# Sixteen rows of the first input pair are loaded ahead of the weights

## The chip, the cores and the metric

The kernel runs on one core of one Trainium2 chip. The metric is the device time of one execution in microseconds; the median of 3 runs of the kernel before is 133.78 us (133.74 to 133.89). The core has TensorE (PE), VectorE (DVE), ScalarE (ACT), GpSimd (POOL) and SyncE (SP), and 16 DMA engines that carry the transfers which SP issues.

## The reference, cut to what matters

The reference is a factorisation machine with a small network on its embedding, for 1024 samples of 12500 features:

```python
x_reg = input_data @ W_lin.T + b_lin                     # (1024, 1)
emb = input_data @ factors                               # (1024, 16)
sum_squared = jnp.square(emb.sum(axis=1))
squared_sum = (jnp.square(input_data) @ jnp.square(factors)).sum(axis=1)
h = jax.nn.relu(emb @ W1.T + b1)                         # 128
h = jax.nn.relu(h @ W2.T + b2)                           # 64
dnn_out = h @ W3.T + b3
x = x_reg + 0.5 * (sum_squared - squared_sum)[:, None] + dnn_out
return (0.5 + jax.nn.sigmoid(x) * 5.0).squeeze()
```

All is float32. The input alone has 1024 x 12500 x 4 = 51.2 MB, and each of its elements is used once as it is and once squared.

## The kernel before, in words

The input is transposed on the host, so that features lie on partitions. 97 chunks of 128 features and a rest of 84 features make up the 12500. The first chunk (`xf`) and the rest (`xl`) are loaded on their own; the other 96 chunks are taken in groups of 8 chunks by 512 samples: first all 12 groups of samples 0 to 511, then 8 groups of samples 512 to 1023, and the last 32 chunks of samples 512 to 1023 in 9 smaller pieces (`x_end`). A group is 128 partitions by 4096 numbers, that is 16 KB to a partition.

For every group ACT and DVE square the 8 chunks (3 by DVE, 5 by ACT; lines 327 and 427) into `sq`, POOL places the weights of the group (lines 307 and 308), and PE multiplies: eight matmuls of the input with `wr` and eight of the squares with `wz`, all adding into one PSUM bank (`add_mm`, line 506). After samples 0 to 511 the small network is run for them while the second half is loaded.

All loads are issued by SP, in the order of the code (lines 265 to 285): the head `hd` (all weights and parameters, 128 rows of 7616 bytes), `xf` (128 rows of 4096 bytes), `xl` (128 rows of 3072 bytes), then eight transfers of two groups each, here called pairs (128 rows of 32 KB, 4 MB), then four single groups and nine end pieces. `xr` has six slots of one group. The first three pairs are issued at once; each later one waits (line 272) until PE has used the squares of the groups whose slots it takes (`sq_used`). In `x_pairs`, row p of a pair holds what goes to partition p.

A transfer adds 16 to its semaphore when it has landed. The three pairs of slots have one semaphore each (`x_landed`), and `landed` (line 231) waits for 16 for each round of the six slots. Before pair 0, PE does 4 matmuls on `xf` and 24 on `xl`, then as many on their squares; they need `hd`, `xf`, `xl` and the sums over squared weights that DVE makes from `hd` (lines 410 to 417).

Of the kernel before, what the change touches and what calls it, by code (L numbers as in the profile page):

```python
# [14 lines left out]
P = 128  # L15
# [9 lines left out]
HALF = B // 2  # L25
CHUNKS = 8
TWO = 2
# [7 lines left out]
PAIRED = 16  # L35
# [10 lines left out]


BY_DVE = 3

# [34 lines left out]
def fm_kernel(nc, head, x_first, x_rest, x_pairs, x_groups, x_end, out):  # L86
    with ExitStack() as ctx:
        def sb(name, shape, dt=F32):
            return ctx.enter_context(nc.sbuf_tensor(name, shape, dt))
# [4 lines left out]
        def sem(name):  # L94
            return ctx.enter_context(nc.semaphore(name))
# [4 lines left out]
        xr = sb("xr", [P, SLOTS, CHUNKS, HALF])  # L100
# [35 lines left out]
        x_landed = [sem(f"x_landed{t}") for t in range(SLOTS // TWO)]  # L136
# [40 lines left out]
        def cols(k):  # L177

            c, n = BLOCKS[k]
            return slice(c, c + n)  # L180
# [16 lines left out]
        def line(k):  # L197

            c, n = BLOCKS[k]
            return slice(c // 4, (c + n) // 4)  # L200
# [8 lines left out]
        def width(i):  # L209
            return BLOCKS[PIECES[i][0]][1]  # L210
# [4 lines left out]
        def piece(i, c, n):  # L215

            at = ENDS * (BLOCKS[PIECES[i][0]][0] - HALF)
            return xe[:, at + c * width(i):at + (c + n) * width(i)]
# [8 lines left out]
        def ring(s):  # L227

            return (s + RING - TOTAL) % RING

        def landed(engine, r, s):

            engine.wait_ge(x_landed[s // TWO], 16 * (r + 1))

        def single(engine, g):
            engine.wait_ge(single_landed[g - PAIRED], 16)
# [1 line left out]
        def chunks(i):  # L238
            return sum(PIECES[i][2]) + sum(PIECES[i][3])

        def last_slot(i):
            k, c = PIECES[i][:2]
            return (ENDS * (BLOCKS[k][0] - HALF) + (c + chunks(i)) * BLOCKS[k][1] - 1) // (CHUNKS * HALF)
# [18 lines left out]

        @block.sync
        def _(sp):
            sp.dma_start(hd[:, :], head).then_inc(hd_landed, 16)  # L265
            sp.dma_start(xf[:, :], x_first).then_inc(first_landed, 16)  # L266
            sp.dma_start(xl[:, :, :].rearrange("p c b -> p (c b)"), x_rest).then_inc(rest_landed, 16)  # L267
            for p in range(PAIRED // TWO):
                at = TWO * p % SLOTS
                if TWO * p >= SLOTS:  # L270

                    sp.wait_ge(sq_used, RING + TWO * p + TWO - SLOTS)
                sp.dma_start(xr[:, at:at + TWO].rearrange("p s c b -> p (s c b)"),  # L273
                             x_pairs[p, :, 0:TWO * CHUNKS * HALF]).then_inc(x_landed[at // TWO], 16)
            for g in range(PAIRED, TOTAL):
                sp.wait_ge(sq_used, RING + g + 1 - SLOTS)
                sp.dma_start(xr[:, g % SLOTS].rearrange("p c b -> p (c b)"),
                             x_groups[g - PAIRED, :, 0:CHUNKS * HALF]).then_inc(single_landed[g - PAIRED], 16)
            at = 0
            for i in range(len(PIECES)):  # L280
                c, n = PIECES[i][1], chunks(i)
                rows = x_end[at:at + P * n * width(i)].rearrange("(p m) -> p m", p=P)
                sp.wait_ge(sq_used, RING + TOTAL - SLOTS + END_SLOT + last_slot(i) + 1)
                sp.dma_start(piece(i, c, n), rows).then_inc(end_landed[i], 16)
                at += P * n * width(i)

            for k in range(len(BLOCKS)):
                sp.wait_ge(y_ready[k], 1)
                sp.dma_start(out[cols(k)].rearrange("(q b) -> q b", q=4), y[0:P:32, line(k)]).then_inc(y_stored, 16)
            sp.wait_ge(y_stored, 16 * len(BLOCKS))  # L290
# [27 lines left out]
        def _(act):  # L318
# [5 lines left out]
            def squares(r, s):  # L324

                act.wait_ge(sq_used, SLOTS * r + s + 1)
                nc.scalar.activation(sq[:, ring(s), BY_DVE:CHUNKS, :], xr[:, s, BY_DVE:CHUNKS, :],  # L327
                                     ACT.Square).then_inc(act_squared, 1)
# [30 lines left out]
            with act.Fori(0, GROUPS // SLOTS) as r:  # L359
                for s in range(SLOTS):  # L360
                    landed(act, r, s)
                    squares(r, s)
# [9 lines left out]
            for g in range(GROUPS, PAIRED):  # L372
                landed(act, g // SLOTS, g % SLOTS)
                squares(g // SLOTS, g % SLOTS)
# [32 lines left out]
        def _(dve):  # L407
# [16 lines left out]
            def squares(r, s):  # L424

                dve.wait_ge(sq_used, SLOTS * r + s + 1)
                nc.vector.tensor_tensor(sq[:, ring(s), 0:BY_DVE, :], xr[:, s, 0:BY_DVE, :], xr[:, s, 0:BY_DVE, :],  # L427
                                        ALU.mult).then_inc(dve_squared, 1)
# [33 lines left out]
            with dve.Fori(0, GROUPS // SLOTS) as r:  # L462
                for s in range(SLOTS):
                    landed(dve, r, s)
                    squares(r, s)
# [38 lines left out]
        def _(pe):  # L504
            def add_mm(out, lhsT, rhs):
                return nc.tensor.matmul(out, lhsT, rhs, start=False, stop=False, skip_group_check=True)  # L506
# [12 lines left out]
            def quad(ps, t, m, c, n):  # L519
                return ps[32 * (t % 4):32 * (t % 4) + m, c:c + n]  # L520
# [29 lines left out]
            def add_squares(r, s, h):  # L550
                g = SLOTS * r + s
                pe.wait_ge(wz_ready, g + 1)
                pe.wait_ge(dve_squared, g + 1)
                for c in range(BY_DVE):
                    add_mm(quad(p_lin[h], c, WZ, 0, HALF), wz[:, ring(s), c, :], sq[:, ring(s), c, :])
                pe.wait_ge(act_squared, g + 1)
                for c in range(BY_DVE, CHUNKS):
                    mm = add_mm(quad(p_lin[h], c, WZ, 0, HALF), wz[:, ring(s), c, :], sq[:, ring(s), c, :])
# [212 lines left out]
```

## Time and profile before

| | us |
|---|---|
| median of 3 runs | 133.78 |
| the profiled execution | 133.76 |
| its span, first to last instruction | 132.0 |
| PE busy | 107.0 |
| ACT busy | 61.5 |
| DVE busy | 52.6 |
| POOL busy | 15.7 |

The span is what the profile's times count; 1.76 us of the profiled execution lie around it. A time such as 17.55 is counted from the start of the span. The DMA share of a stretch is the mean busy share of the 16 DMA engines; a packet is put down to where it starts, so that a short stretch can show more than 1.00. In the timelines, instructions of one line that follow each other are merged into a row, and the bracket says how long the engine stood idle before it and what ended that. The loads move 52.22 MB.

### The profile page before, as it was taken

The numbers are of one execution on the slowest core, as the hardware profiler recorded it, in microseconds if no ns is written. First come the engines' busy times: TensorE is split into PE (matmuls) and PEld (weight loads), VectorE is DVE, ScalarE is ACT, GpSimd is POOL, SyncE is SP. The second block draws the span as 40 slices with busy tenths as digits, with TensorE's granted clock in tenths as the row PEclk, the third lists the DMA queues.
The fourth block names the chain that finished last, engine by engine and source line by source line (L and its number), as shares of the span: only waits on it lengthen the run. The fifth ranks groups of instructions, "written<-read, shape, count | busy, mean of one in ns | idle before, by whom it ended". The sixth has DMA issues, their size and how long they took to land.

```text
span 132.0 us, 2607 instructions
## 1 busy us (share of the span) xinstructions
PE 107.0 (81%) x1123; PEld 34.6 (26%) x1123; DVE 52.6 (40%) x51; ACT 61.5 (47%) x52; POOL 15.7 (12%) x48
## 2 busy tenths in 40 slices
PE   6099969429979839749749979999998987989992
PEld 4012222002212112112112233322222112345881
DVE  0391063027036036046045016565351351576571
ACT  4030067029039039049048046868562561465851
POOL 3015000200010200200200110164530000000000
PEclk9999999995999999999977999999999999999999
DMA  3999899989999998998999999899999999999700
GB/s 106 413 531 417 377 477 472 407 387 467 427 387 462 457 427 387 457 437 387 467 457 427 387 457 447 377 432 412 452 407 407 462 415 417 418 404 411 302 26 1
DMA packets 3489, 52.36 MB, mean 397 GB/s; under 512 B 404, under 2 KB 536, under 8 KB 1560
## 3 DMA queue, kind: packets, MB, share of 16 engines
q1 hardware_dynamic: 3480, 52.23, 93.2%
q8 instruction: 7, 0.11, 0.4%
q14 instruction: 2, 0.02, 0.0%
HBM read 52.22 MB, written 0.00 MB: 396 GB/s over the span
## 4 chain that ended last, share of the span: by engine, by line
DMA 54%; PE 40%; SPq 2%; DVE 1%; issue 1%; ACT 1%
DMA xr<-in_x_pairs 43%; PE p_lin L506 34%; DMA xr<-in_x_end 11%; PE p_sq L506 2%; PE p_h L601 2%; SPq L273 1%; PE p_tot L506 1%; PE p_h L632 1%; PE p_tot L614 0%; DVE h L454 0%; DVE h L449 0%; SPq L267 0%; SPq L266 0%; PE p_tot L621 0%; SPq L265 0%
## 5 line engine op out<-in xcount | busy, mean ns | idle before, releaser
L327 ACT ACTIVATE sq<-xr 128x2560 f32<-128x2560 f32 x20 | 45.9, 2333 | 46.8 <-DMA xr<-in_x_pairs 38.8
L427 DVE TENSOR_TENSOR sq<-xr 128x1536 f32<-128x1536 f32 x20 | 34.6, 1761 | 53.7 <-DMA xr<-in_x_pairs 42.9
L506 PE MATMUL p_lin<-xr,wr 128*17 128x512 f32 x320 | 39.9, 638 | 15.6 <-DMA xr<-in_x_pairs 14.4
L506 PE MATMUL p_lin<-sq,wz 128*18 128x512 f32 x320 | 37.7, 592 | 0.0
L506 PEld LDWEIGHTS p_lin<-xr,wr 128*17 128x17 f32 x320 | 9.2, 102 | 44.5 <-issue 38.4
L307 POOL COPY wr<-hd 128x136 f32 (+1 forms) x20 | 9.3, 464 | 75.0 <-PE p_lin L506 75.0
L506 PEld LDWEIGHTS p_lin<-sq,wz 128*18 128x18 f32 x320 | 10.1, 98 | 25.8 <-issue 25.0
L506 PE MATMUL p_lin<-xr,hd 128*17 128x352 f32 (+1 forms) x128 | 10.0, 380 | 1.3 <-DMA xr<-in_x_end 1.3
L437 DVE TENSOR_TENSOR sq<-xr 128x1408 f32<-128x1408 f32 (+3 forms) x6 | 6.6, 1135 | 6.1 <-DMA xr<-in_x_end 6.1
L337 ACT ACTIVATE sq<-xr 128x1408 f32<-128x1408 f32 (+3 forms) x6 | 5.7, 983 | 6.3 <-DMA xr<-in_x_end 6.3
L506 PE MATMUL p_lin<-sq,ws 128*18 128x352 f32 x64 | 6.6, 459 | 0.0
L506 PE MATMUL p_lin<-xf,hd 128*17 128x512 f32 x4 | 3.6, 1046 | 3.4 <-DMA xf<-in_x_first 3.4
L506 PEld LDWEIGHTS p_lin<-xr,hd 128*17 128x17 f32 x128 | 4.3, 97 | 5.2 <-issue 3.3
L308 POOL COPY wz<-s_all 128x8 f32 (+1 forms) x20 | 5.5, 273 | 0.0
L437 DVE TENSOR_TENSOR xr<-xr 128x320 f32<-128x320 f32 (+1 forms) x9 | 3.7, 451 | 2.2 <-DMA xr<-in_x_end 2.1
L506 PE MATMUL p_sq<-xr,ws 128*18 128x160 f32 x64 | 4.0, 300 | 0.0
L337 ACT ACTIVATE xr<-xr 128x320 f32<-128x320 f32 (+1 forms) x9 | 3.4, 432 | 0.9 <-DMA xr<-in_x_end 0.8
L449 DVE TENSOR_SCALAR h<-p_h,hd 128x256 f32<-128x256 f32 (+1 forms) x2 | 0.9, 434 | 6.9 <-PE p_h L601 6.8
L410 DVE SCALAR_TENSOR_TENSOR fsq<-hd 128x1552 f32<-128x1552 f32 x1 | 1.8, 1774 | 4.4 <-DMA hd<-in_head 4.4
L322 ACT ACTIVATE sqf<-xf 128x1024 f32<-128x1024 f32 x1 | 1.1, 1057 | 4.6 <-DMA xf<-in_x_first 4.6
L341 ACT COPY lin<-p_lin 128x256 f32<-128x256 f32 (+1 forms) x4 | 1.2, 342 | 4.2 <-PE p_lin L506 4.1
L506 PEld LDWEIGHTS p_lin<-sq,ws 128*18 128x18 f32 x64 | 2.4, 97 | 2.4 <-issue 1.4
(52 smaller groups left out, 40.8 us busy)
## 6 DMA issues: line engine op xcount, KB each, us to landing
xr<-in_x_pairs SPq DMA_DIRECT2D x8, 4096.0 KB, 21.9
xr<-in_x_groups SPq DMA_DIRECT2D x4, 2048.0 KB, 18.3
xr<-in_x_end SPq DMA_DIRECT2D x1, 2112.0 KB, 10.5
xr<-in_x_end SPq DMA_DIRECT2D x3, 640.0 KB, 12.0
xr<-in_x_end SPq DMA_DIRECT2D x1, 1760.0 KB, 14.3
xr<-in_x_end SPq DMA_DIRECT2D x1, 1056.0 KB, 12.4
hd<-in_head SPq DMA_DIRECT2D x1, 952.0 KB, 4.8
xr<-in_x_end SPq DMA_DIRECT2D x1, 704.0 KB, 13.7
```

Source lines behind the costliest of these rows:

```text
L273: sp.dma_start(xr[:, at:at + TWO].rearrange("p s c b -> p (s c b)"), x_pairs[p, :, 0:TWO * CHUNKS * HALF]).then_inc(x_landed[at // TWO], 16)
L307: nc.gpsimd.tensor_copy(wr[:, ring(s), :, :], w[:, bass.ds(at, CHUNKS), :]).then_inc(wr_ready, 1)
L308: nc.gpsimd.tensor_copy(wz[:, ring(s), :, LIN:WZ].rearrange("p c k -> p (c k)"), s_all[:, bass.ds(at, CHUNKS)]).then_inc(wz_ready, 1)
L327: nc.scalar.activation(sq[:, ring(s), BY_DVE:CHUNKS, :], xr[:, s, BY_DVE:CHUNKS, :], ACT.Square).then_inc(act_squared, 1)
L337: nc.scalar.activation(squared_piece(i, c, n), piece(i, c, n), ACT.Square).then_inc(act_end_squared, 1)
L341: nc.scalar.copy(lin[:, part(k, u)], p_lin[k][:, u * BLOCKS[k][1] // 2:(u + 1) * BLOCKS[k][1] // 2]).then_inc(lin_ready[k], 1)
L410: nc.vector.scalar_tensor_tensor(fsq[:, :, :], w[:, :, 0:EMB], -0.5, w[:, :, 0:EMB], ALU.mult, ALU.mult).then_inc(fsq_ready, 1)
L427: nc.vector.tensor_tensor(sq[:, ring(s), 0:BY_DVE, :], xr[:, s, 0:BY_DVE, :], xr[:, s, 0:BY_DVE, :], ALU.mult).then_inc(dve_squared, 1)
L437: nc.vector.tensor_tensor(squared_piece(i, c, n), piece(i, c, n), piece(i, c, n), ALU.mult).then_inc(dve_end_squared, 1)
L506: return nc.tensor.matmul(out, lhsT, rhs, start=False, stop=False, skip_group_check=True)
L601: mm = nc.tensor.matmul(bank[32 * t:32 * t + 32, 0:n], pr[:, C_W1 + 32 * t:C_W1 + 32 * t + 32], rhs, start=True, stop=True, skip_group_che ...
L632: mm = nc.tensor.matmul(p_h2[32 * t:32 * t + 32, row(k)], pr[:, C_W2 + t % 2 * 32:C_W2 + t % 2 * 32 + 32], h1[:, part(k, t // 2)], start=T ...
```

## The change

Pair 0 is split. A first transfer, ahead of `hd`, loads 16 rows of 32 KB into partitions 0 to 15 of slots 0 and 1. A second, behind `xl`, loads the other 112 rows into partitions 16 to 127. Both add 16 to the semaphore of the first two slots, so every wait for these slots asks for 16 more. The remaining pairs are as before.

In memory the rows of pair 0 are put in another order: row 8g (g from 0 to 15) holds what goes to partition g, and rows 8g+1 to 8g+7 hold what goes to partitions 16+7g to 22+7g. The first transfer thus reads every eighth row, and the second seven neighbouring rows and then skips one.

```diff
--- before.py
+++ after.py
@@ -46,6 +46,11 @@
 
 
 BY_DVE = 3
+
+
+
+AHEAD = 16
+EVERY = P // AHEAD
 
 
 
@@ -230,7 +235,7 @@
 
         def landed(engine, r, s):
 
-            engine.wait_ge(x_landed[s // TWO], 16 * (r + 1))
+            engine.wait_ge(x_landed[s // TWO], 16 * (r + 1) + (16 if s < TWO else 0))
 
         def single(engine, g):
             engine.wait_ge(single_landed[g - PAIRED], 16)
@@ -262,10 +267,14 @@
 
         @block.sync
         def _(sp):
+            slot = xr[:, 0:TWO].rearrange("p s c b -> p (s c b)")
+            pair = x_pairs[0, :, 0:TWO * CHUNKS * HALF].rearrange("(g r) m -> g r m", r=EVERY)
+            sp.dma_start(slot[0:AHEAD, :], pair[:, 0, :]).then_inc(x_landed[0], 16)
             sp.dma_start(hd[:, :], head).then_inc(hd_landed, 16)
             sp.dma_start(xf[:, :], x_first).then_inc(first_landed, 16)
             sp.dma_start(xl[:, :, :].rearrange("p c b -> p (c b)"), x_rest).then_inc(rest_landed, 16)
-            for p in range(PAIRED // TWO):
+            sp.dma_start(slot[AHEAD:P, :], pair[:, 1:EVERY, :]).then_inc(x_landed[0], 16)
+            for p in range(1, PAIRED // TWO):
                 at = TWO * p % SLOTS
                 if TWO * p >= SLOTS:
 
@@ -737,6 +746,8 @@
             x_pairs[g // TWO, :, at:at + CHUNKS * HALF] = rows
         else:
             x_groups[g - PAIRED, :, :CHUNKS * HALF] = rows
+    x_pairs[0] = np.concatenate([x_pairs[0, :AHEAD, None], x_pairs[0, AHEAD:].reshape(AHEAD, EVERY - 1, -1)],
+                                axis=1).reshape(P, -1)
     ends = chunks[ALL - 1 - ENDS:]
     x_end = np.concatenate([ends[c:c + sum(a) + sum(d), :, BLOCKS[k][0]:sum(BLOCKS[k])].transpose(1, 0, 2).ravel()
                             for k, c, a, d in PIECES])
```

On SP, at the start of the program, before the change (`hd` are the weights, `xr` the slots of the input):

```order
L265 DMA hd<-in_head 128x1904
L266 DMA xf<-in_x_first 128x1024
L267 DMA xl<-in_x_rest 128x768
L273 DMA xr<-in_x_pairs 128x8192 x3
L273 DMA xr<-in_x_pairs 128x8192 [waits sq_used] x5
L277 DMA xr<-in_x_groups 128x4096 [waits sq_used] x4
```

The same place in the changed kernel, where 16x8192 and 112x1x8192 are the two parts of pair 0:

```order
L272 DMA xr<-in_x_pairs 16x8192
L273 DMA hd<-in_head 128x1904
L274 DMA xf<-in_x_first 128x1024
L275 DMA xl<-in_x_rest 128x768
L276 DMA xr<-in_x_pairs 112x1x8192
L282 DMA xr<-in_x_pairs 128x8192 x2
L282 DMA xr<-in_x_pairs 128x8192 [waits sq_used] x5
L286 DMA xr<-in_x_groups 128x4096 [waits sq_used] x4
```

SP issues one transfer more; `hd`, `xf` and `xl` each stand one place later, and behind pair 0 nothing moves. The engines that compute keep their instructions and their order.

## Rows read from the trace of the kernel before

**Rows 1.** The page, section 2: the span in 40 slices, DMA busy tenths and GB/s.
```profile
DMA  3999899989999998998999999899999999999700
GB/s 106 413 531 417 377 477 472 407 387 467 427 387 462 457 427 387 457 437 387 467 457 427 387 457 447 377 432 412 452 407 407 462 415 417 418 404 411 302 26 1
```

**Rows 2.** Stretches of 20 us: length, busy by engine, PE clock, DMA share, GB/s.
```profile
4.00:24.00 20.00, 15.79 (x116) 4.00 (x120) 8.14 (x8) 5.62 (x3) 2.62 (x10) 1.00 1.03 442
...
44.00:64.00 20.00, 14.65 (x140) 3.87 (x136) 6.86 (x4) 9.13 (x4) 2.19 (x10) 1.00 1.00 429
...
104.00:124.00 20.00, 18.11 (x240) 7.43 (x238) 10.00 (x11) 9.94 (x15) 0.00 (x0) 1.00 1.00 417
```

**Rows 3.** The page, section 3: DMA queues, packets, MB, share of 16 engines.
```profile
q1 hardware_dynamic: 3480, 52.23, 93.2%
q8 instruction: 7, 0.11, 0.4%
```

**Rows 4.** Timeline of ACT: start, us, line, operation [idle before <-releaser].
```profile
17.55 4.57 ACT L327 ACTIVATE sq<-xr 128x2560 f32<-128x2560 f32 x2 [9.69 <-DMA xr<-in_x_pairs]
28.74 4.57 ACT L327 ACTIVATE sq<-xr 128x2560 f32<-128x2560 f32 x2 [6.62 <-DMA xr<-in_x_pairs]
38.45 4.57 ACT L327 ACTIVATE sq<-xr 128x2560 f32<-128x2560 f32 x2 [5.14 <-DMA xr<-in_x_pairs]
48.20 4.57 ACT L327 ACTIVATE sq<-xr 128x2560 f32<-128x2560 f32 x2 [5.17 <-DMA xr<-in_x_pairs]
```

**Rows 5.** DMA queue of instructions between the landing of pair 0 and of pair 1.
```profile
q8 instruction: 1, 0.02, 0.6%
```

**Rows 6.** Timeline of PE near the end.
```profile
106.58 1.91 PE L506 MATMUL p_lin<-xr,wr 128*17 128x512 f32 x16 [0.63 <-DMA xr<-in_x_groups]
...
115.86 1.66 PE L506 MATMUL p_lin<-xr,hd 128*17 128x352 f32 x18 [0.39 <-DMA xr<-in_x_end]
```

**Rows 7.** Timeline of SP at the start: DMA issues.
```profile
0.74 0.39 SPq L265 DMA_DIRECT2D hd<-in_head  x1
1.20 0.41 SPq L266 DMA_DIRECT2D xf<-in_x_first  x1
1.64 0.43 SPq L267 DMA_DIRECT2D xl<-in_x_rest  x1
2.12 1.78 SPq L273 DMA_DIRECT2D xr<-in_x_pairs  x3
```

**Rows 8.** Stretches of 0.5 us at the start, columns as in rows 2.
```profile
1.50:2.00 0.50, 0.50 (x4) 0.33 (x3) 0.00 (x0) 0.50 (x1) 0.27 (x1) 1.00 1.00 122
2.00:2.50 0.50, 0.50 (x5) 0.36 (x3) 0.00 (x0) 0.22 (x2) 0.00 (x0) 1.00 0.31 76
2.50:3.00 0.50, 0.50 (x4) 0.38 (x3) 0.00 (x0) 0.00 (x0) 0.00 (x0) 1.00 0.72 259
3.00:3.50 0.50, 0.50 (x3) 0.02 (x1) 0.00 (x0) 0.00 (x0) 0.00 (x0) 1.00 1.02 426
```

**Rows 9.** DMA issues of the whole span: KB each, us from issue to landing.
```profile
hd<-in_head SPq DMA_DIRECT2D x1, 952.0 KB, 4.8
...
xf<-in_x_first SPq DMA_DIRECT2D x1, 512.0 KB, 5.6
...
xl<-in_x_rest SPq DMA_DIRECT2D x1, 384.0 KB, 6.1
```

**Rows 10.** Timeline of PE up to pair 1.
```profile
6.92 3.57 PE L506 MATMUL p_lin<-xf,hd 128*17 128x512 f32 x4 [3.41 <-DMA xf<-in_x_first]
...
14.80 1.49 PE L506 MATMUL p_lin<-sql,ws 32*18 32x256 f32 x24
17.58 3.63 PE L506 MATMUL p_lin<-xr,wr 128*17 128x512 f32 x32 [1.29 <-DMA xr<-in_x_pairs]
...
28.76 1.74 PE L506 MATMUL p_lin<-xr,wr 128*17 128x512 f32 x12 [4.12 <-DMA xr<-in_x_pairs]
```

## The prediction

> **What bounds the kernel now.** I read the slices first. From the second slice to the 37th the DMA engines stand at 8 or 9 tenths [rows 1]; the reader should see that no slice there falls below. Stretches of 20 us sharpen it: a DMA share of 1.03, 1.00 and 1.00 at 442, 429 and 417 GB/s [rows 2], and the load queue alone fills 93.2% of the span with its 52.23 MB [rows 3]. So this is a load-bound kernel: at about 430 GB/s, 26.9 GB/s for each of 16 engines, the bytes set the time. ACT's timeline shows the same as a pace: pairs 1, 2 and 3 start at 28.74, 38.45 and 48.20, 9.71 and 9.75 us apart [rows 4]. A pair is 8 rows of 32 KB for each engine, so one row costs an engine 9.71/8 = 1.21 us.
>
> Then the timeline of PE, to see whether a shift of the loads reaches the end. At 106.58 and at 115.86 PE still waits 0.63 and 0.39 us for data [rows 6]. Everything behind 115.86 hangs on landings, so what the loads lose or gain goes one to one into the end.
>
> One more thing stands in ACT's pace: between pairs 0 and 1 lie 28.74 - 17.55 = 11.19 us, 1.48 more than the regular 9.71 [rows 4], and in that time one packet of the instruction queue was carried [rows 5]; there are 7 of them [rows 3]. A transfer lands when its last engine is done, so engines that carry instructions besides are late, and the end belongs to such an engine.
>
> **The change part by part.** *One transfer more on SP.* An issue costs 0.39 to 0.43 us (0.74, 1.20, 1.64) [rows 7]. `hd`, `xf` and `xl` are issued one place, 0.45 us, later, but the engines have 1.21 us of row each meanwhile: nothing for the end. It costs up to 0.45 us if the first rows didn't cover it.
>
> *The start.* The first issue begins at 0.74 [rows 7] and the engines have packets from about 1.5. Full rate is there at 3.0 (426 GB/s); from 1.5 to 3.0 the rates are 122, 76 and 259 GB/s [rows 8]. Those three stretches move (122 + 76 + 259) x 0.5 us = 229 KB, which takes 0.53 us at 430: 0.97 us are lost. In the first stretch the engines are busy (1.00) and wait for their first data, which stays. In the next two the share is 0.31 and 0.72, so (0.69 + 0.28) x 0.5 = 0.49 us of an engine's time has no packet. With one long row each, handed out first, the engines should all be at work early, and later packets be ready in time. Bounds: a gain between nothing and 0.49 us. I take the middle, 0.25 us.
>
> *Where the sixteen rows go.* Every load of the kernel before spans all 128 partitions; 16 engines then move 16 x 26.9 GB/s. The trace does not tell whether 26.9 is what an engine can carry or what a path into the memory can take, since with 128 partitions both are 16. If it is the path, each serves 128/16 = 8 partitions, and the first transfer, all on 16 neighbouring partitions, can't use them all. Bounds: one row to each path costs no more than the row's own 1.21 us; with eight neighbours to a path, all 16 rows go through two paths, 8 x 1.21 = 9.7 us, 8.5 more. Between them, with two or four neighbours on a path, it is 2 or 4 rows in turn. I take four: 3 x 1.21 = 3.64 us more, the middle one of the three cases with sharing. While it lasts, the packets of `hd` stand behind the rows in each engine's line, so every engine is set back.
>
> The Trainium skill, "SBUF — State Buffer", section "Door 1: The DMA port swizzle (why `[64,N]` ≈ `[32,N]`)", says that four neighbouring partitions share one of 16 write ports and gives 104 GB/s for a load into partitions 0 to 15. By that figure the 512 KB would take an estimated 5.0 us in place of 1.21. No run here shows it yet.
>
> *The other 112 rows.* They are 7 for each engine, written to partitions 16+7g to 22+7g, and so no longer in the places that a 128-partition load gives each engine. If paths are shared, at least one path must take eight rows while an engine has seven, 1.21 us more; at most every one of the seven is shared by two engines, 7 x 1.21 = 8.5 us. The middle is 4.86. From it I take the 1.48 us by which the engine that sets the end is late already [rows 4], because the engine held up here need not be one that carries instructions: 3.38 us.
>
> *What is behind `hd`.* `hd`, `xf` and `xl` land 4.8, 5.6 and 6.1 us after their issue [rows 9], and PE works from 6.92 until 14.80 + 1.49 = 16.29 on what they bring, then waits 1.29 us for pair 0 [rows 10]. With the sharing all of them move by 1.21 + 3.64 - 0.25 = 4.6 us, PE's start to 11.5 and its end to 20.9; pair 0 then lands at 17.55 + 6.8 = 24.3, so PE waits longer there. Without sharing PE is done at 16.29 + 0.96 = 17.25, still ahead of pair 0 at 17.3. Either way 4.12 us of waiting before pair 1 [rows 10] absorbs the rest. Without that cover it would be up to 1 us.
>
> Sum: 133.76 - 0.25 + 3.64 + 3.38 = 140.53, from the profiled execution, 0.02 us below the median of 133.78. I forecast 140.5 us.
>
> **The rivals.** *No sharing: only the start moves.* The 26.9 GB/s belong to the engine, and any 16 rows load at full rate. For it speaks that the rate is the same in every stretch, whatever the row's length [rows 2]; nothing in the trace of before speaks against it. Then only the start counts: 133.76 - 0.25 = 133.5, by its bounds 133.3 to 133.8. Faster than before or level, where I forecast slower.
>
> *Only the sixteen rows share.* The 112 rows spread so evenly that no two engines meet, or those that meet are not the ones that set the end: 133.76 - 0.25 + 3.64 = 137.1. For it speaks that 7 of 8 rows of each engine come in a transfer almost as wide as before.
>
> *The change does not do what it says.* The 16 rows are carried by few engines, say four with four rows each, and these have fewer of the 112. Each engine's total is then as before: 133.8, with `hd` late and nothing else. If the totals don't even out, it is again 3.64 more. The row on `hd` shows only the whole transfer, not its split.
>
> The Trainium skill, "DMA: Bandwidth & Descriptors", section "Why a DMA increments its semaphore by 16 and not by 1", states that a transfer is divided over the largest number of engines up to 16 that divides the outer dimension on both sides, here 16 both times; by it this last rival falls. The rows here show no engine by itself.
>
> **How the numbers follow.** Forecast (both parts share): 44%, its own range 138.5 to 142.5. No sharing: 31%. Only the sixteen rows: 17%. Not as it says: 8%. A measurement here tells no change from about 0.2%, 0.27 us. Without sharing the gain of 0 to 0.49 us lies on either side of that bound: 16 of the 31 to faster, 14 to no change, 1 to slower. Of the 8, 7 go to no change and 1 to slower, rounded with the rest: faster 0.16, same 0.21, slower 0.63. The range must hold both signs: from 133.2, just below the largest gain (133.76 - 0.49 = 133.27), to 142.5, the forecast and 2 us more. Above it lie sharing by eight (145 and more) and seven rows that all share.
>
> **What would show it.** Right: the first transfer takes four times 1.21 us, `hd` lands at about 10 us on the span's clock in place of 5.5, DMA rates near 110 to 200 GB/s in stretches before it, and pair 0 starts on ACT near 24 us; from pair 1 on the pace is 9.7 us again, and the end is as late as pair 1. If pair 0 is only 3.4 us later than 17.55, the 112 rows did not share. Wrong: `hd` lands at 6.5 us, rates are at 430 GB/s from 2.5 us on, and pair 0 starts at 17.3. A change of pace behind pair 1, or PE no longer waiting at the end, would be none of these.

## The result and the profile after

The changed kernel takes 143.34 us (143.30 to 143.60, 4 runs) against 133.81 us, the median of the kernel before over 4 runs; the ratio is 1.0716, with a 95% interval of 1.0698 to 1.0735. It is slower by 9.5 us. Forecast were 140.5 us in a range up to 142.5: the direction was right, the size too small, and the time lies outside the range.

The slices of the changed kernel, columns as in [rows 1]:

```profile
DMA  9499998899999999999999999989999999999800
GB/s 148 62 392 376 277 250 213 296 434 439 434 444 444 444 434 411 444 407 416 416 434 434 444 444 444 444 370 421 439 416 421 430 436 421 412 407 411 334 28 1
```

The DMA engines are as busy as before, at 8 or 9 tenths from the third slice on, but in the fifth to the eighth slice they move 277, 250, 213 and 296 GB/s. Here a busy share says that packets are under way, not how fast they move. The stretches, columns as in [rows 2]:

```profile
4.00:24.00 20.00, 7.82 (x56) 1.90 (x56) 4.71 (x6) 1.06 (x1) 2.19 (x8) 1.00 0.99 273
...
44.00:64.00 20.00, 16.17 (x136) 3.88 (x132) 6.86 (x4) 9.13 (x4) 2.13 (x10) 0.91 1.02 438
...
104.00:124.00 20.00, 17.88 (x164) 4.95 (x160) 7.70 (x5) 9.14 (x6) 1.67 (x4) 1.00 1.00 423
```

273 GB/s in place of 442 in the first stretch, and the old rates behind it. Everything that was lost was lost before pair 1. The timeline of ACT, to be laid beside [rows 4], and of PE near the end, beside [rows 6], say the same:

```profile
27.74 4.57 ACT L336 ACTIVATE sq<-xr 128x2560 f32<-128x2560 f32 x2 [15.58 <-DMA xr<-in_x_pairs]
38.60 4.57 ACT L336 ACTIVATE sq<-xr 128x2560 f32<-128x2560 f32 x2 [6.29 <-DMA xr<-in_x_pairs]
48.32 4.57 ACT L336 ACTIVATE sq<-xr 128x2560 f32<-128x2560 f32 x2 [5.15 <-DMA xr<-in_x_pairs]
```

```profile
116.40 1.91 PE L515 MATMUL p_lin<-xr,wr 128*17 128x512 f32 x16 [0.62 <-DMA xr<-in_x_groups]
...
125.69 1.66 PE L515 MATMUL p_lin<-xr,hd 128*17 128x352 f32 x18 [0.40 <-DMA xr<-in_x_end]
```

Pair 0 starts 27.74 - 17.55 = 10.19 us late, pair 1 38.60 - 28.74 = 9.86, and near the end it is 116.40 - 106.58 = 9.82 and 125.69 - 115.86 = 9.83. The span grew from 132.0 to 141.8; the profiled execution took 143.60 us, 0.26 above the median, so that the profile shows 9.8 us where the medians show 9.5. PE waits 0.62 and 0.40 us in the same places as before: the loss at the start is carried to the end unchanged.

The issues up to 30 us, KB each, and us from issue to landing, as in [rows 9]:

```profile
xr<-in_x_pairs SPq DMA_DIRECT2D x1, 3584.0 KB, 25.1
hd<-in_head SPq DMA_DIRECT2D x1, 952.0 KB, 8.6
xr<-in_x_pairs SPq DMA_DIRECT2D x1, 512.0 KB, 6.9
xf<-in_x_first SPq DMA_DIRECT2D x1, 512.0 KB, 9.5
xl<-in_x_rest SPq DMA_DIRECT2D x1, 384.0 KB, 10.2
```

The sixteen rows (512 KB from `in_x_pairs`) and `xf` are the same size. Between the landings of `hd` and `xf` lies 1.3 us; the sixteen rows need 6.9 us from their issue. The start in half microseconds, as in [rows 8]:

```profile
1.50:2.00 0.50, 0.50 (x4) 0.33 (x3) 0.00 (x0) 0.50 (x1) 0.27 (x1) 1.00 5.71 786
2.00:2.50 0.50, 0.50 (x5) 0.35 (x3) 0.00 (x0) 0.22 (x2) 0.00 (x0) 1.00 1.93 262
...
3.00:3.50 0.50, 0.50 (x3) 0.03 (x1) 0.00 (x0) 0.00 (x0) 0.00 (x0) 1.00 0.00 0
...
5.00:5.50 0.50, 0.00 (x0) 0.00 (x0) 0.00 (x0) 0.00 (x0) 0.00 (x0) 1.00 0.73 76
```

A packet counts where it starts. All sixteen rows start before 2.5 us (786 and 262 GB/s, for half a microsecond each, are 524 KB, the whole transfer), then nothing starts for more than 2 us. The records of these packets last 3.3 to 4.5 us, median 3.76. The trace also has the increments of the transfer's semaphore one by one, sixteen for a transfer, read here as one from each engine: they come between 6.98 and 7.62 us. PE up to pair 1, beside [rows 10]:

```profile
11.22 3.17 PE L515 MATMUL p_lin<-xf,hd 128*17 128x512 f32 x4 [7.72 <-DMA xf<-in_x_first]
...
17.55 1.49 PE L515 MATMUL p_lin<-sql,ws 32*18 32x256 f32 x24
27.76 5.17 PE L515 MATMUL p_lin<-xr,wr 128*17 128x512 f32 x32 [8.72 <-DMA xr<-in_x_pairs]
...
38.62 3.63 PE L515 MATMUL p_lin<-xr,wr 128*17 128x512 f32 x32 [2.25 <-DMA xr<-in_x_pairs]
```

PE is done with its first work at 19.04 and waits 8.72 us for pair 0. From `xl` to pair 0 the 112 rows take the time: between 12 and 24 us the loads run at this rate:

```profile
12.00:24.00 12.00, 7.04 (x56) 1.77 (x54) 2.56 (x4) 0.17 (x1) 2.19 (x8) 1.00 1.00 254
```

254 GB/s at a full share; the 112 packets last 1.67 to 2.38 us each, median 2.06, in place of 1.21. Not one of them is as short as a row was before. Pair 0's last sixteen increments come at 16.98 to 17.45 us before and at 26.06 to 27.64 in the changed kernel: every engine is held up, by 8.6 us or more.

### The profile page after: what moved, and what is told of

Read it like the earlier page. It is cut to its first block, busy times and chain, and to the rows that moved or that the text cites. A ratio compares the mean times of both kernels' runs of the same rounds, so it can differ in the third digit from the quotient of the medians.

```text
span 141.8 us, 2608 instructions
## 1 busy us (share of the span) xinstructions
PE 107.0 (75%) x1123; PEld 34.5 (24%) x1123; DVE 52.5 (37%) x51; ACT 61.5 (43%) x52; POOL 12.7 (9%) x48
## 4 chain that ended last, share of the span: by engine, by line
DMA 65%; PE 31%; SPq 2%; issue 1%; ACT 0%; DVE 0%
DMA xr<-in_x_pairs 54%; PE p_lin L515 27%; DMA xr<-in_x_end 10%; PE p_sq L515 1%; PE p_h L610 1%; SPq L276 1%; PE p_tot L515 0%; PE p_tot L623 0%; SPq L275 0%; SPq L274 0%; SPq L273 0%; SPq L272 0%; PE p_tot L630 0%; SPq L293 0%; ACT sg L365 0%
## 5 line engine op out<-in xcount | busy, mean ns | idle before, releaser
L515 PE MATMUL p_lin<-xr,wr 128*17 128x512 f32 x320 | 41.4, 658 | 21.2 <-DMA xr<-in_x_pairs 19.9
L316 POOL COPY wr<-hd 128x136 f32 (+1 forms) x20 | 7.8, 390 | 83.5 <-PE p_lin L515 83.5
L317 POOL COPY wz<-s_all 128x8 f32 (+1 forms) x20 | 3.9, 197 | 0.0
```

What stands on the lines that cost most here:

```text
L316: nc.gpsimd.tensor_copy(wr[:, ring(s), :, :], w[:, bass.ds(at, CHUNKS), :]).then_inc(wr_ready, 1)
L317: nc.gpsimd.tensor_copy(wz[:, ring(s), :, LIN:WZ].rearrange("p c k -> p (c k)"), s_all[:, bass.ds(at, CHUNKS)]).then_inc(wz_ready, 1)
```

## The experiments

All times stand beside the kernel before at medians of 133.80 to 133.82 us. Where no interval is given, a kernel was executed once; the kernel before spread over 133.58 to 134.01. Each transfer that is added, or that pair 0 is cut into, counts on the semaphore of slots 0 and 1, and `landed` asks for 16 more for each, as in the change.

**The same bytes ahead, but on all partitions.**

```diff
+            sp.dma_start(slot[:, 0:1024], x_pairs[0, :, 0:1024]).then_inc(x_landed[0], 16)
             sp.dma_start(hd[:, :], head).then_inc(hd_landed, 16)
...
+            sp.dma_start(slot[:, 1024:8192], x_pairs[0, :, 1024:8192]).then_inc(x_landed[0], 16)
+            for p in range(1, PAIRED // TWO):
```

> The first transfer carries the same 512 KB ahead of the weights, but as 128 rows of 4 KB: 1024 numbers of every partition of pair 0; the other 7168 follow behind xl. Theory (neighbouring partitions share a write path): all paths are used, so the first transfer takes 1.21 us of transfer time as any 512 KB did before, hd lands at about 5.0 + 1.2 = 6.2 us, pair 0 on ACT at 17.5, total 133.8 (133.4 to 134.1). Rival (anything long ahead of the weights sets the rest back, or the split of the pair costs by itself): hd at 9 us and a total of 138 or more.

133.83 us, ratio 1.0001 (0.9991 to 1.0011). Issue to landing, and pair 0 on ACT:

```profile
hd<-in_head SPq DMA_DIRECT2D x1, 952.0 KB, 5.6
xr<-in_x_pairs SPq DMA_DIRECT2D x1, 512.0 KB, 3.7
```

```profile
17.63 4.57 ACT L330 ACTIVATE sq<-xr 128x2560 f32<-128x2560 f32 x2 [8.50 <-DMA xr<-in_x_pairs]
```

512 KB ahead of the weights, a pair cut in two, one more transfer and a longer wait: all that costs nothing. It gains nothing either.

**Both parts behind the weights.** The line of the 16 rows is moved to directly ahead of that of the 112 rows.

```diff
-            sp.dma_start(slot[0:AHEAD, :], pair[:, 0, :]).then_inc(x_landed[0], 16)
             sp.dma_start(hd[:, :], head).then_inc(hd_landed, 16)
...
+            sp.dma_start(slot[0:AHEAD, :], pair[:, 0, :]).then_inc(x_landed[0], 16)
             sp.dma_start(slot[AHEAD:P, :], pair[:, 1:EVERY, :]).then_inc(x_landed[0], 16)
```

> The two parts of pair 0, 16 rows and 112 rows, are kept, memory order too, but both are issued behind xl; the weights come first as before. Theory (paths shared by neighbouring partitions): the place in the queue does not matter, both parts share as before; hd lands at 5.0 us, pair 0 starts on ACT near 27 us, total 143 (142 to 144). Rival (the order is what costs): total 133.8 to 134.5.

144.80 us, with `hd` on time and pair 0 late:

```profile
hd<-in_head SPq DMA_DIRECT2D x1, 952.0 KB, 4.6
```

```profile
28.79 4.57 ACT L336 ACTIVATE sq<-xr 128x2560 f32<-128x2560 f32 x2 [20.99 <-DMA xr<-in_x_pairs]
```

The order is not what costs. It is even 1.5 us worse here, 0.8 above the range expected. The sixteen rows take 3.27 to 4.91 us and sixteen of the 112 packets take 2.7 to 4.0, so that the two transfers seem to run into each other; how these add up was not taken apart.

**Two halves of 64 partitions.**

```diff
+            for q in range(2):
+                sp.dma_start(slot[64 * q:64 * q + 64, :], x_pairs[0, 64 * q:64 * q + 64, 0:TWO * CHUNKS * HALF]).then_inc(x_landed[0], 16)
```

> Pair 0 in two transfers of 64 partitions (0 to 63, 64 to 127), both behind xl, memory as before the change. Theory (paths shared): if 64 partitions reach half of the paths, each engine's 4 rows of a half go two to a path and take 8 x 1.21 us; both halves 19.4 us in place of 9.7: pair 0 lands 9.7 us late, packets take 2.4 us each, total 143.5 (142 to 144.5). Rival (the memory order of the rows, or a 16-row transfer, is what costs): neither is here, total 133.8 to 134.2.

144.44 us, 0.9 us more than expected. The stretch in which the halves are loaded:

```profile
8.00:26.00 18.00, 7.57 (x56) 1.68 (x53) 2.21 (x4) 0.00 (x0) 2.17 (x8) 0.78 0.99 204
```

204 GB/s is a little under half of 430, at a full share; the median packet is 2.57 us, 2.1 times 1.21. No 16-row transfer and no new memory order are in this kernel. 64 partitions thus reach about half of the paths. The Trainium skill, "SBUF — State Buffer", section "Door 1: The DMA port swizzle (why `[64,N]` ≈ `[32,N]`)", lists 196 GB/s for partitions 0 to 63 at 1 MiB; the 204 GB/s here, in a stream of 2 MB transfers, are 4% more.

**Rows of pair 0 in memory as before.** `pair` is here `x_pairs[0]` as it lies, without the new order on the host.

```diff
-            sp.dma_start(slot[0:AHEAD, :], pair[:, 0, :]).then_inc(x_landed[0], 16)
+            sp.dma_start(slot[0:AHEAD, :], pair[0:AHEAD, :]).then_inc(x_landed[0], 16)
...
-            sp.dma_start(slot[AHEAD:P, :], pair[:, 1:EVERY, :]).then_inc(x_landed[0], 16)
+            sp.dma_start(slot[AHEAD:P, :], pair[AHEAD:P, :]).then_inc(x_landed[0], 16)
```

> The change with the rows of pair 0 left in memory in the order of the partitions: the first transfer reads 16 neighbouring rows, the second the 112 behind them. Theory (paths shared on the writing side): nothing moves, 143.3 (142.8 to 143.8), first packets 3.3 to 4.5 us. Rival (reading every eighth row, 264 KB apart, is what is slow): the first transfer falls to 1.2 to 2 us and the total to 134 to 139.

143.32 us, the first packets 3.2 to 4.0 us. The order of the rows in memory does nothing that shows in the time.

**Sixteen rows added to the kernel before, in four placements.** They go to a buffer that is free then and are used by nothing; pair 0 stays whole. The partitions alone differ:

```diff
+            spare = sq[:, 0:TWO].rearrange("p s c b -> p (s c b)")
+            sp.dma_start(spare[0:16, :], x_pairs[0, 0:P:8, 0:TWO * CHUNKS * HALF]).then_inc(x_landed[0], 16)
             sp.dma_start(hd[:, :], head).then_inc(hd_landed, 16)
```

> The kernel before, its pair 0 whole as it was, plus an additional transfer of 16 rows of 32 KB ahead of the weights, into partitions 0 to 15 of a buffer that is free then. It prices the first transfer of the change alone. Theory (four neighbours share a path): hd lands 4.1 us later, at 9.1, pair 0 is as regular as before, total 133.8 + 4.1 = 137.9 (137.5 to 138.7). So of the 9.5 us of the change some 5.5 to 6.7 would belong to the 112 rows. Rival (what costs is that pair 0 is cut in two): the additional 0.5 MB cost 1.21 us and the total is 135.0.

> As the run with neighbours, but the 16 rows go to partitions 32, 36, ..., 92. Theory (groups of four neighbours, of which p and p + 32 have one path): now each row has a path of its own; first packets take 1.21 us and the wait for first data, about 2 us together, hd lands at 6.2, total 133.8 + 1.21 = 135.0. If the start gains from one long row for each engine as forecast, it is 0.25 (0 to 0.49) less: 134.8 (134.5 to 135.0). Rival (a transfer of 16 rows, or of every eighth row in memory, is slow wherever it goes): 137.9.

> As the run with neighbours, but the rows go to partitions 0, 4, ..., 60. Theory (p and p + 32 have one path): two rows to a path, first packets near 3.2 us, hd at 7.5, total 133.8 + 2.5 = 136.3 (136.0 to 136.7). Rival (only neighbours within 4 or 8 partitions share): hd at 6.2, total 135.0.

> As the run with neighbours, but the rows go to partitions 28, 32, ..., 88, of which only 28 and 60 should share a path. It asks why the 112 rows cost more than my middle value. If sharing holds up only the two engines concerned: 14 first packets near 2.0 us and 2 near 3.2. If engines hinder each other beyond the shared path (their transfers stand behind one another on the way there): most of the 16 packets take clearly over 2.0 us, up to 3.2. Total 135.0 to 136.3 in either case.

Issue to landing of the added transfer, in this order: neighbours, 32 to 92 in steps of 4, 0 to 60 in steps of 4, 28 to 88 in steps of 4:

```profile
sq<-in_x_pairs SPq DMA_DIRECT2D x1, 512.0 KB, 6.9
```

```profile
sq<-in_x_pairs SPq DMA_DIRECT2D x1, 512.0 KB, 4.1
```

```profile
sq<-in_x_pairs SPq DMA_DIRECT2D x1, 512.0 KB, 5.2
```

```profile
sq<-in_x_pairs SPq DMA_DIRECT2D x1, 512.0 KB, 5.1
```

| partitions | rows to a path | median packet, us | semaphore's increments, us | total, us | over before, us |
|---|---|---|---|---|---|
| 0, 1, ..., 15 | 4 | 3.64 | 6.57 to 7.66 | 138.02 | 4.2 |
| 0, 4, ..., 60 | 2 | 2.34 | 5.37 to 5.92 | 136.32 | 2.5 |
| 28, 32, ..., 88 | 1, one path 2 | 1.99 | 14 at 4.35 to 5.05, 5.48, 5.86 | 135.69 | 1.9 |
| 32, 36, ..., 92 | 1 | 1.86 | 4.18 to 4.84 | 135.35 | 1.5 |

The Trainium skill, "SBUF — State Buffer", section "Door 1: The DMA port swizzle (why `[64,N]` ≈ `[32,N]`)", gives 104 GB/s for partitions 0 to 15, which made an estimated 5.0 us of the neighbours. Here they make the kernel 4.2 us longer, somewhat less than by the page.

The same rows, the same bytes, the same place in the queue: only the destination differs, and the time goes with the number of rows to a path. One thing differs besides. The issue of the added transfer, first with neighbours, then with 32 to 92 in steps of 4:

```profile
0.74 0.40 SPq L266 DMA_DIRECT2D sq<-in_x_pairs  x1
```

```profile
0.74 0.62 SPq L266 DMA_DIRECT2D sq<-in_x_pairs  x1
```

To issue a transfer to partitions in steps takes 0.22 us longer, and its first packet starts at 2.13 us in place of 1.77. The three placements in steps have this 0.36 us in their totals. The ratio of the spread version is 1.0116 (1.0099 to 1.0134), which is 1.3 to 1.8 us for 1.21 of data and 0.36 of a late start. Its `hd` lands 5.8 us after an issue at 1.42, that is 1.7 us later than before, again 1.21, 0.36 and 0.1 more. So no gain at the start is seen from one long row for each engine, even where no path is shared.

I expected packets near 3.2 us where two rows share a path; with all in pairs the median is 2.34, with one pair the longest is 2.40. The landings come nearer: the last increment is 1.1 us later with two rows to a path than with one, about a row's 1.21, so a packet's record seems not to cover all of its time. That the total of 0, 4, ..., 60 was as expected is partly luck, as 0.36 of its 2.5 us is the late start.

**Why the 112 rows cost more than forecast.** Two more placements of the added rows, in steps of 7, from 16 and from 11 (`spare[16:122:7, :]` and `spare[11:117:7, :]` in the line above):

> The kernel before with an additional transfer of 16 rows ahead of the weights, to partitions 16, 23, ..., 121: the places at which the 16 engines would begin the 112 rows if each takes seven neighbours. Theory A (each engine seven neighbours, paths by fours, p and p + 32 together): only 16 and 51, and 72 and 107, share; 12 first packets near 1.9 us, 4 near 2.4, hd 1.3 to 2.1 us late, total 135.3 to 136.3. Theory B (sharing hits more engines than these paths say): most packets near 2.4 or longer, as in the 112 rows, total 136.3 or more.

> As the run with every seventh partition, but from 11 on: 11, 18, ..., 116, which by the same paths are 16 different ones. Theory A: like partitions 32, 36, ..., 92: first packets near 1.9 us, total 135.3. Theory B (the paths are others): packets of 2.3 us and more, total 136.3 or more.

```profile
sq<-in_x_pairs SPq DMA_DIRECT2D x1, 512.0 KB, 5.2
```

```profile
sq<-in_x_pairs SPq DMA_DIRECT2D x1, 512.0 KB, 4.2
```

From 16: 136.26 us, median packet 2.16. From 11: 135.37 us, median 1.84. Steps of 7 are no trouble by themselves, and the sixteen paths fit the theory. The landing at 5.2 says little of the others: a transfer lands with its last engine, and one shared path was enough for 5.1. The single packets say more. From 16, ten of sixteen took more than 2.1 us, and from 11 the longest took 2.02; the median increment is at 5.4 us, with all in pairs at 5.6, with none shared at 4.5. By the theory only four engines share, so engines that share nothing were held up too.

The 112 rows as seven transfers:

```diff
-            sp.dma_start(slot[AHEAD:P, :], pair[:, 1:EVERY, :]).then_inc(x_landed[0], 16)
+            for j in range(1, EVERY):
+                sp.dma_start(slot[AHEAD - 1 + j:P:EVERY - 1, :], pair[:, j, :]).then_inc(x_landed[0], 16)
```

> The change with the 112 rows issued as seven transfers of 16 rows: the j-th takes the j-th of the seven rows of each group, partitions 15+j, 22+j, ... . If an engine takes seven neighbours in the one transfer of 112 rows, this hands out the same rows to the same engines in the same order: 143.3 (142.8 to 144.0), packets near 2.0 us. If the transfer of 112 rows is divided in another way that collides more, this is faster: the 16 rows cost 2.9 us, the seven rows 1.2 to 4.9, total 138 to 141.5.

143.74 us, median packet 2.08 against 2.06. This fits that in the one transfer each engine takes seven neighbours, as assumed. If so, and if the engines kept in step, only 24 of the 112 rows would meet another on a path of the theory. If these alone were held up, the others would still take 1.21 us, but the shortest of the 112 took 1.67.

A shared path that lasts:

```diff
+            sp.dma_start(spare[28:92:4, :], x_pairs[0, 0:P:8, 0:TWO * CHUNKS * HALF]).then_inc(x_landed[0], 16)
+            sp.dma_start(spare[29:93:4, :], x_pairs[0, 1:P:8, 0:TWO * CHUNKS * HALF]).then_inc(x_landed[0], 16)
...
             sp.dma_start(hd[:, :], head).then_inc(hd_landed, 16)
```

> The kernel before with four additional transfers of 16 rows ahead of the weights, to partitions 28, 32, ..., 88, then 29, 33, ..., and so on: 14 engines with a path of their own, two (28 and 60) that share for four rows on end. Additional data 2 MB, 4.86 us. If sharing holds up only the two: 14 engines are done with hd at 5.0 + 4.9 = 9.9 us, two at about 13 to 14.7, and the total is 142 to 143.5, since a transfer lands with its last engine. If engines hinder each other: most engines late, hd packets spread evenly between 10.5 and 14.7, the four rows at clearly over 1.3 us each for all.

143.98 us, above the 142 to 143.5 of two engines held up alone. The stretch from 4 to 12 us:

```profile
4.00:12.00 8.00, 0.00 (x0) 0.00 (x0) 0.00 (x0) 0.00 (x0) 0.00 (x0) 1.00 0.96 268
```

If two engines halved one path and 14 went on, 15 x 26.9 = 404 GB/s would be left. It is 268. In the second of the four rows exactly two packets are long (2.55 us); from the third on many others are as well. Twelve packets start between 5.0 and 6.3 us, while the two engines that share are still at their second row, and eight of the twelve take 1.33 to 2.34 us. All twelve are over by 7.8, and the first packet of `hd` starts only at 8.27, so these engines were not held up by others that were at `hd` already; behind that, this can be a part. The engines do hinder each other beyond the shared path, here from the third row on. Where on the way this happens no run shows.

## Why the prediction was right in kind and wrong in size

- **The bound and the way to the end: right.** Pair 1, the waits near the end and the span are late by the same 9.8 to 9.9 us, and PE still waits in the same places.
- **One transfer more on SP at nothing: right** (133.83 us with the same number of transfers on all partitions).
- **The start, a gain of 0.25 us: wrong, it is none.** With all partitions the ratio is 1.0001; with a row on its own path for each engine the added 512 KB cost 1.5 us, and the 0.3 above 1.21 is the late start of that transfer (0.36). The interval of that run alone, 1.3 to 1.8 us against 1.57, would still allow 0.25; its `hd`, 0.1 us later than without a gain, speaks against it.
- **Sixteen rows, 3.64 us more, four to a path: right in kind and near in size.** From its rows the prediction took four as the middle of three cases; the placements now show it. Alone they cost 4.2 - 1.21 = 3.0 us. That includes the start; forecast for both together were 3.64 - 0.25 = 3.39.
- **The 112 rows, 3.38 us: this term failed.** What is left of the total is 9.53 - 3.0 = 6.5 us, almost twice the term; the packets alone make 7 x (2.06 - 1.21) = 6.0. Two steps made it too small. The first is the deduction of 1.48 us, for which the engine held up by the rows had to be another than the one that carries instructions. The reading behind it was right: of pair 1's increments before the change, fifteen come at 26.69 to 27.16 us and one at 28.64. But all sixteen engines were held up, that one too; its increment is the last again, at 38.50, 9.86 us later. Between pair 0 and pair 1 only 10.19 - 9.86 = 0.33 us came back. The second is the middle, 4.86 between 1.21 and 8.5, for which no row spoke. It was too small because engines that share nothing do not go on at full rate: the shortest of the 112 packets, the run with two shared paths and that with a lasting pair show it. Where they hinder each other stays open.
- **What is behind `hd`, at nothing: right.** PE was done with its first work at 19.04 us, earlier than the 20.9 forecast, and waited 8.72 us for pair 0.
- **The rivals.** No sharing at all falls with the four placements. Only the sixteen rows share (137.1): the added neighbours alone, at 138.02 less 1.21, come to 136.8, so this was its price, but the 112 rows share as well. Fewer engines for the 16 rows: 16 packets start between 1.5 and 2.5 us and all overlap, and the sixteen increments come one by one from 6.98 to 7.62 us; both fit an engine for each row.
- **The range** ended at 142.5, two above the forecast, while the text itself named seven rows that all share. With the bound of that term in it, it would have reached 133.76 - 0.25 + 3.64 + 8.5 = 145.7 and held the time.

## What to carry to other kernels

In a load-bound kernel, a transfer is judged by where its rows land at the same moment, not by whether every DMA engine has one: sixteen engines on 16 neighbouring partitions added 4.2 us for 512 KB, sixteen rows with a path each 1.5 us. To bring a part of a tile ahead, cut its columns and keep all 128 partitions; here that costs nothing. A busy share of 9 tenths with fallen GB/s was the mark of it in this profile.

## What the runs showed of the hardware that was not expected

- Two shared paths of sixteen held up nearly all engines of a transfer: the median increment came at 5.4 us, with eight shared paths at 5.6, with none at 4.5. One pair that lasted four rows brought the load rate between 4 and 12 us to 268 GB/s, from about 430.
- Sixteen engines share fully on 64 partitions, and each packet then takes 2.57 us, 6% more than twice 1.21.
- The issue of a 16-row transfer to partitions in steps of 4 took 0.62 us on SP, that to neighbours 0.40, and its first packet started 0.36 us later.
- With one packet for each engine the first packets still start over 0.50 us in the changed kernel (1.75 to 2.25) and over 0.83 us with the added neighbours, against 0.77 us with eight packets for each before: this spread does not come from the number of packets.
